# Row maxima of a guard job's four heads: one VectorE reduction over both PSUM banks, where there were two of one bank each

## The reference

```python
Q, K, V = (proj(Wq, bq), proj(Wk, bk), proj(Wv, bv))
Kg = K[:, :, idx]; Vg = V[:, :, idx]              # 32 listed keys for each query
s_scores = jnp.einsum('bhsd,bhskd->bhsk', Q, Kg) * scale
s_scores = jnp.where(prior_index_mask, s_scores, -jnp.inf)
sparse_out = jnp.einsum('bhsk,bhskd->bhsd', jax.nn.softmax(s_scores, axis=-1), Vg)
```

## Time and profile before

| | |
|---|---|
| Median of three runs | 498.06 us (496.38 to 498.22) |
| The profiled execution | 495.82 us |
| Its span, first to last instruction | 493.9 us |
| PE busy | 458.7 us (93%), 2479 instructions |
| DVE busy | 387.2 us (78%), 763 instructions |
| ACT busy | 257.9 us (52%), 506 instructions |
| Mean granted TensorE clock | 0.992 |

### The profile page before, as it was taken

One profiled execution on the slowest core, in us unless ns is written; L12 is line 12 of the kernel. 1 busy time (PEld: TensorE's weight loads), 2 busy tenths in 40 slices (PEclk: granted clock), 3 DMA queues, 4 the chain that ended last, 5 costly groups with the idle time before them and its releaser, 6 DMA issues.

```text
span 493.9 us, 7595 instructions
## 1 busy us (share of the span) xinstructions
PE 458.7 (93%) x2479; PEld 319.0 (65%) x2479; DVE 387.2 (78%) x763; ACT 257.9 (52%) x506; POOL 91.6 (19%) x97
## 2 busy tenths in 40 slices
PE   4998989999999999897999999999999999999990
PEld 2445554454545454445888888888888878899980
DVE  4997989999899989884877578747883679475377
ACT  3016478778878785873534453445353524365500
POOL 3003100101110113000100004500450024067720
PEclk9999999999999999999999999999999999999996
DMA  7900020799600000002251210111020101646358
GB/s 224 233 29 1 0 87 1 267 326 338 218 1 0 1 1 2 0 1 86 54 128 44 84 45 21 66 42 44 19 70 0 44 19 68 171 138 206 121 190 272
DMA packets 24095, 45.25 MB, mean 92 GB/s; under 512 B 7938, under 2 KB 17794, under 8 KB 23778
## 3 DMA queue, kind: packets, MB, share of 16 engines
q1 hardware_dynamic: 21410, 37.46, 24.7%
q0 software_dynamic: 2640, 7.24, 4.1%
HBM read 35.29 MB, written 23.00 MB: 118 GB/s over the span
## 4 chain that ended last, share of the span: by engine, by line
PE 45%; DVE 2%; DMA 2%; POOL 1%; issue 1%; ACT 0%; SPq 0%; DVEq 0%; POOLq 0%
PE psG L1660 5%; PE psG L1662 5%; PE psG L1661 5%; PE psS L1660 4%; PE psS L1662 4%; PE psS L1661 4%; PE psO L1660 2%; PE psO L1662 2%; PE psO L1661 2%; PE psM L1660 2%; PE psM L1662 2%; PE psM L1661 2%; DVE attT L1971 1%; POOL expert_rows L1887 1%; DMA expert_rows<-crow,place_in 1%
## 5 line engine op out<-in xcount | busy, mean ns | idle before, releaser
L699 ACT ACTIVATE Pr<-psS 128x512 f32<-128x512 f32 x128 | 69.9, 603 | 33.6 <-PE psS L556 33.1
L783 DVE SCALAR_TENSOR_TENSOR Pr<-Pr,few_W 128x1024 f32<-128x1024 f32 x64 | 80.8, 1269 | 2.0 <-ACT Pr L699 1.8
L775 DVE TENSOR_REDUCE few_Qa<-psG 128x2 fp32r<-128x512 f32 x116 | 74.5, 686 | 5.6 <-PE psG L541 5.3
L539 PE MATMUL psG<-few_KG,QG 128*128 128x512 f32 x116 | 53.0, 501 | 3.2 <-DVE few_Qa L775 3.1
L556 PE MATMUL psS<-few_QAT,few_KP 128*128 128x512 f32 x128 | 48.1, 451 | 4.2 <-ACT Pr L699 2.7
L1911 DVE TENSOR_TENSOR hT_lo<-V,hT_hi 128x512 fp32r<-128x512 f32 x64 | 44.5, 695 | 2.2
L541 PE MATMUL psG<-Mneg,few_identb 128*128 128x512 bf16 x116 | 45.2, 390 | 0.0
L1909 DVE CAST hT_hi<-V 128x512 fp32r<-128x512 f32 x64 | 27.5, 430 | 18.0 <-ACT V L1846 11.1
L405 POOL TENSOR_TENSOR few_Qa<-Qn,few_Qa 128x256 fp32r<-128x256 f32 x16 | 16.4, 1028 | 125.3 <-ACT few_Qa L641 125.3
L556 PEld LDWEIGHTS psS<-few_QAT,few_KP 128*128 128x128 f32 x128 | 20.6, 190 | 26.6 <-issue 19.8
L1865 POOL TENSOR_TENSOR cT_lo<-attT,cT_hi 128x1024 fp32r<-128x1024 f32 x4 | 10.6, 2656 | 132.9 <-ACT cT_hi L1796 132.9
(11 more groups left out here) (302 smaller groups left out, 1151.3 us busy)
## 6 DMA issues: line engine op xcount, KB each, us to landing
expert_rows<-blank_dram SPq DMA_DIRECT2D x8, 1548.0 KB, 23.7
block_rows<-expert_rows SPq DMA_DIRECT2D x31, 129.0 KB, 2.3
back<-expert_results SPq DMA_DIRECT2D x6, 512.0 KB, 6.4
staged<-w_dram SPq DMA_DIRECT2D x4, 512.0 KB, 4.6
x1T<-xT_dram SPq DMA_DIRECT2D x4, 512.0 KB, 4.4
staged<-ew_dram SPq DMA_DIRECT2D x4, 512.0 KB, 3.2
few_idxb<-entries_by_query SPq DMA_DIRECT2D x8, 192.0 KB, 7.9
out_dram<-attT SPq DMA_DIRECT2D x6, 256.0 KB, 2.6
```

The source lines that it names most:

```text
L539: nc.tensor.matmul(o, QG[:, (u // 2) % 2, st * P:st * P + P], self.KG[:, u % 2, 2 * p:2 * p + 2, :], start=True, stop=False)
L699: nc.scalar.activation(Pr[:, i % JOBS, 512 * f:512 * f + 512], psS[:, f, :], ACT.Exp, scale=SCALE).then_inc(self.s["s_exp"], 1)
L775: nc.vector.tensor_reduce(self.Qa[:, f % SLOTS, st, 2 * p:2 * p + 2, 48], self.guard_bank(i)[0][:, p, :].rearrange("p (h t) -> p h t", h=2 ...
L783: nc.vector.scalar_tensor_tensor(pr, pr, FMAX, self.W[:, r, :], ALU.min, ALU.mult).then_inc(self.s["s_prob"], 1)
```

## The change

One `tensor_reduce` over the four heads of both banks takes the place of the loop over two banks. It waits until both banks are complete, writes four maxima for each query where each of the two wrote two, and raises `g_max` by two at its end. The values written are the same, and nothing else is changed; TensorE's waits on `g_max` stand as they were.

```diff
@@ -770,11 +770,11 @@
-                        for p in range(2):
-                            dve.wait_ge(self.s["g_scores"], 2 * i + p + 1)
-                            nc.vector.tensor_reduce(self.Qa[:, f % SLOTS, st, 2 * p:2 * p + 2, 48],
-                                                    self.guard_bank(i)[0][:, p, :].rearrange("p (h t) -> p h t", h=2), AX.X,
-                                                    ALU.max, negate=True).then_inc(self.s["g_max"], 1)
+
+                        dve.wait_ge(self.s["g_scores"], 2 * i + 2)
+                        scores = self.guard_bank(i)[0][:, :, :].rearrange("p k n -> p (k n)").rearrange("p (h t) -> p h t", h=HG)
+                        nc.vector.tensor_reduce(self.Qa[:, f % SLOTS, st, :, 48], scores, AX.X,
+                                                ALU.max, negate=True).then_inc(self.s["g_max"], 2)
```

## The result

| | before | after |
|---|---|---|
| Median | 497.37 us (4 runs, 496.38 to 498.22) | 512.91 us (4 runs, 511.57 to 514.78) |
| The profiled execution | 495.82 us | 514.78 us |
| First to last reduction of the guard jobs | 150.9 us | 167.3 us |
| From the last reduction to the end of the span | 294.5 us | 297.3 us |
| Instructions on DVE | 763 | 699 |

The changed kernel is slower: the ratio of the times is 1.0322, with a 95% interval of 1.0289 to 1.0355. VectorE's busy time hardly moved (387.1 us in place of 387.2), though 64 instructions are gone and the guard jobs' reductions are busy for 78.4 us in place of 82.2. Busy time counts overlapping instructions once; added up one by one, VectorE's instructions take 411.2 us in place of 421.9, so they now overlap less.

The account below looks back on a forecast made before the run. In the guard-job stage VectorE was taken to lead, with TensorE close to its limit. +11.9 us for 51 periods, +1.3 opening, +0.4 job 12 and -0.2 end gave +13.4: 511.5 us from 498.06, range 505.0 to 516.0.

Parts of the forecast that it names:

- The instruction: Joined reduction on VectorE: 1.22 us long, occupying 1.13 against 1.20 for the pair; bounds 1.08 and 1.29 us.
- The ring: Short guard jobs: reduction and guard matmuls wait for each other in turn, 2.66 us a job instead of 2.33.
- The jobs that TensorE fills: Guard jobs where TensorE's own work sets the time: six at 3.16, six at 3.00, five at 3.39 us.
- The opening and job 12: Start of the guard stage: jobs 0 to 11 lose 1.3 us, job 12's wait for its second bank 0.4.
- The waits: VectorE's wait for mask matmuls grows from 5.3 to about 20 us, TensorE's for the reduction from 3.1 to over 12.
- The weighings: VectorE's weighings in the guard stage: of 3.1 us of delay, part is swallowed by slack; 1.7 us counted.
- signs of being wrong: Guard stage: short jobs staying at 2.3 us, reduction under 1.1 or over 1.3 us, or granted clock falling.
- Behind the stage: After the last guard reduction: the stretch to the end keeps its length.
- DVE as the limit (faster): Guard stage: TensorE is late anyway, so the later release costs nothing; 4.5 us saved, 493.6 us; chance 4%.
- the grouping half of the Trainium skill's rule: Guard-stage reductions: grouping into larger operations helps where the engine is saturated; would give -4.5 us.
- the dearer instruction: Two-bank reduction costs what the pair does, 1.29 us; +2.7 us, 514.2 us; chance 10%, counted as slower.
- The clock rival: Guard stage: more idle time drops TensorE's clock to its lower level; 41 us more, some 552 us; chance 2%.

Follow-up runs that it names:

- e7: Changed kernel with GpSimd's subtraction for the dense layer held back until the last guard maximum; 510.61 us, ratio 1.0271.
- e1: Kernel before, still two reductions, but the first also waits for both banks, each freeing its own; 504.15 us, ratio 1.0146.
- e5: Kernel before with the one two-bank reduction in jobs 0 to 11 only; 499.01 us, ratio 1.0037.
- e2: Kernel before, two reductions starting as before, but only the second frees both banks; 501.26 us, ratio 1.0083.
- e3: Kernel before, two reductions that both wait for both banks, only the second freeing them; 512.66 us, ratio 1.0329.
- e6: Kernel before with the one two-bank reduction from job 12 on only; 513.26 us, ratio 1.0312.
- e4: Changed kernel with its reduction reading only the first 128 of each head's 256 keys; 496.12 us, ratio 0.9982.

## Why the prediction was right

The direction, the mechanism and the size held: 511.5 us were forecast in a range of 505 to 516, 512.91 were measured; +13.4 us were forecast, the median moved by +15.5 and the profiled execution by +19.0. The traces exaggerate: the changed kernel's is its slowest execution (514.78), that of the kernel before is faster than all four of its timed runs. The forecast also started from the median of three runs, 498.06, which became 497.37 with a fourth; that brings it 0.7 us nearer by chance.

- *The instruction.* 1.22 us were taken from L760 and L783, 1225 ns were measured. The bounds of 1.08 and 1.29 us weren't needed.
- *The ring.* 2.66 us were worked out, 2.63 to 2.68 measured in nearly every short job ahead of the slow spot (two took 2.71 and 2.72).
- *The jobs that TensorE fills.* 3.16, 3.00 and 3.39 were carried over; 3.20, 2.98 and 3.42 were measured, in the jobs that the order in `due` named, but for one: job n = 10 took 2.63. It stands right behind the weight splitting of job 21, which took 3.75 us in place of the 3.39 worked out, so the two misses nearly cancel (that of job 12 took 2.88, 2.86 worked out). Two jobs with four more transposes took 2.99 and 2.98 us, the rest left at the floor stayed there.
- *The opening and job 12.* +1.3 and +0.4 worked out; +1.65 and +0.44 measured. Where job 7's guard matmuls have key transposes ahead of them on TensorE, one period of 1.58 us stands between the 1.13 and 1.50 of the plain ring, and the opening ends on a period of 1.50, where the sum ended on one of 1.13.
- *The waits.* About 20 us in some 50 places for VectorE, over 12 us for TensorE: 21.2 us in 44, and 16.1.
- *The weighings: this term was mis-sized.* Its 1.7 us of delay were thought of as a share that the slack would not swallow. The slack swallowed nearly all of the small delays (the weighings of 1.39 us leave the period at 2.67), but one collision with GpSimd, which cost a weighing 1.0 us before, cost 2.0, and behind it TensorE stood idle and then ran at the lower of its clock's two levels from 209.5 to 212.9 us. In place of 1.7 stand some 3.2 us, all in the last three periods; e7, which removes them, has 51 periods of 146.2 us together against 145.3 in the sum without this term. A fall of the clock in the stage was one of the prediction's own signs of being wrong; it came, but it is part of these 3.2 us and not the cause of the other 11, as e7 shows, which has none.
- *Behind the stage.* The stretch after the last reduction is 2.8 us longer, not of equal length as forecast. In that execution the clock shows a second fall there. Over the kernels whose program behind the stage is that of before, this stretch takes 294.3 to 295.7 us in the traces without such a fall ahead of the last work (before, e1, e5), 296.6 to 297.3 with one (the change, e2, e3, e6) and 297.6 with two (e4, whose median is no slower than before). So the 2.8 us go with the fall and not with the ring; why the clock falls in one trace and not in another stays open.
- *The rivals.* DVE as the limit (faster) needed 1.87 us of TensorE's work between nearly all guards; the short jobs don't have it, and TensorE waits there as worked out. So the grouping half of the Trainium skill's rule (Perfetto Trace Analysis, Optimizing Scalar/DVE Operations) misled here, at 22.84 of 24 us busy: grouping cost 3.2%; e3 against the change shows only 0.4 us for it in 48 periods at equal waits. The price of the dearer instruction, +2.7 us for the pair's 1.29, did not show in e3, where the pair starts 0.03 to 0.07 us sooner; no run has a two-bank instruction of that length. The clock rival was priced as a fall throughout the stage, which didn't come; a fall of a few microseconds did.

## What to carry to other kernels

Before two instructions are joined, ask what each of them frees and when: a reduction bank by bank lets the producer refill one bank while the other is read, and joining them turns two half steps that overlap into a ring in which each engine waits out the other in full. Add up that ring (produce, signal, consume, signal) and compare it with the period that the fuller engine has today; the saved overhead (0.07 us a job here) is small against what the overlap gave (0.3 us). That an engine is 95% busy doesn't make its instruction overhead the thing to save, when the next engine is right behind it: in e4, with reductions of half the length, 0.8 us in 135 were won.

## What had not been expected of the hardware

- A weighing was held up by 2.0 us when it started 0.24 us after a GpSimd instruction of 2.38 us, and not at all when it started 0.05 us before one. The GpSimd instruction still had 2.14 us to run; where it still had 1.10 (in the kernel before, at 194.92), the weighing was held up by 1.0.
- After 2.63 us without a matmul TensorE's granted clock fell to the lower of its two levels in the changed kernel (209.5 to 212.9 us: 0.57 on average over 209 to 213), and a guard matmul took 0.73 us in place of 0.47. In e1 it fell during a wait of 2.38 us at the same place, and in e3 a wait of 2.67 us there was followed by matmuls of 0.47 us. What makes the difference stays open.
- A reduction over two banks started 0.50 or 0.53 us after the mask matmul's start, the first of the pair in e3 0.43 or 0.49 us; that stays open too.
